# Attention pieces laid out afresh over the steps of a hand-ordered four-layer kernel

## The reference

```python
x = x + _L0(_gn(x))   # triplet attention: max and mean pools along three axes, 7x7 convolutions
                      # of them, sigmoid gates, the three gated branches weighted by a softmax
x = x + _L1(_gn(x))   # 3x3 convolution 256 -> 256, weights mixed from circulant projections
x = x + _L2(_gn(x))   # squeeze and excite: mean of a wavelet low band, two small matrices, sigmoid
x = x + _L3(_gn(x))   # shifted 8x8 window attention, 8 heads of 32, relative bias, mask
```

## Time and profile before

| | us |
|---|---|
| median of 3 runs | 3209.29 (3207.8 to 3211.7) |
| profiled execution | 3209.59 |
| its span | 3207.5 |
| PE, DVE, ACT, POOL busy | 2517.5, 2317.2, 1714.9, 1407.3 |
| mean granted clock of TensorE | 0.92 of full |

### The profile page before, as it was taken

How to read it: one execution, slowest core, us unless ns; L and a number is a source line. 1 busy time by engine, 2 the same in 40 slices (tenths; PEclk the granted TensorE clock), 3 DMA queues, 4 the chain that set the end, 5 groups by cost and what they waited for, 6 DMA issues and landing times. The chain is left out here.

```text
span 3207.5 us, 68136 instructions
## 1 busy us (share of the span) xinstructions
PE 2517.5 (78%) x27316; PEld 1422.3 (44%) x27316; DVE 2317.2 (72%) x4411; ACT 1714.9 (53%) x4448; POOL 1407.3 (44%) x1052
## 2 busy tenths in 40 slices
PE   0266769897888879798888979898788969798666
PEld 0232345444544446444544446444544445444343
DVE  4968676867778786878778786877678786776433
ACT  0221066545664476645764476635765376645765
POOL 4314552456335562456335562456435452454222
PEclk9977879998999989998999979998999989999899
DMA  5300310014000321014000321014010231011100
GB/s 149 104 2 14 108 58 28 21 60 145 28 28 27 118 68 41 21 60 145 28 28 27 103 83 41 21 60 145 22 34 27 73 113 41 21 47 54 41 28 34
DMA packets 91345, 184.50 MB, mean 58 GB/s; under 512 B 37510, under 2 KB 50454, under 8 KB 80406
## 3 DMA queue, kind: packets, MB, share of 16 engines
q1 hardware_dynamic: 88854, 177.78, 16.6%
q10 hardware_dynamic: 2176, 2.36, 0.3%
HBM read 107.23 MB, written 72.86 MB: 56 GB/s over the span
## 5 line engine op out<-in xcount | busy, mean ns | idle before, releaser
L1828 PE MATMUL F<-g_raw,cw_hi 128*128 128x512 f16 x2304 | 714.3, 393 | 62.0 <-DVE ytj L1361 25.5
L821 POOL TENSOR_TENSOR xs<-xs,rec 128x512 f32<-128x512 f32 x256 | 291.2, 1142 | 911.5 <-DVE rec L1615 910.8
L1081 ACT ACTIVATE xs<-xs,mx 128x64 f32<-128x64 f32 x2048 | 513.0, 336 | 166.4 <-DVE mx L1610 166.3
L1828 PE MATMUL F<-g_raw,cw_lo 128*128 128x512 f16 x1152 | 450.7, 391 | 0.0
L1828 PEld LDWEIGHTS F<-g_raw,cw_hi 128*128 128x128 f16 x2304 | 225.6, 100 | 342.9 <-issue 35.8
L1599 DVE TENSOR_TENSOR xs<-SP,bias 128x512 f32<-128x512 f32 (+2 forms) x384 | 182.1, 502 | 199.4 <-PE SP L1904 194.7
L1872 PE MATMUL QP<-tok_hi,qkv_hi 128*128 128x512 f16 x512 | 209.0, 408 | 98.2 <-DVE tok_lo L1584 44.9
L830 POOL TENSOR_TENSOR ot_lo<-ot,ot_hi 128x512 f16<-128x512 f32 x128 | 149.3, 1187 | 263.7 <-ACT ot_hi L1102 263.7
L1334 DVE SCALAR_TENSOR_TENSOR g_raw<-l0c,gn,g_raw 128x512 f16<-128x512 f32 x192 | 199.4, 1083 | 87.3 <-ACT g_raw L965 87.3
L965 ACT ACTIVATE g_raw<-l0c,gn 128x512 f16<-128x512 f32 x192 | 128.1, 716 | 232.2 <-DVE l0c L1327 83.3
L1614 DVE TENSOR_REDUCE sums<-xs 128x8 f32<-128x512 f32 x256 | 172.0, 672 | 89.6 <-ACT xs L1081 87.7
(11 more groups left out here) (268 smaller groups left out, 5798.2 us busy)
## 6 DMA issues: line engine op xcount, KB each, us to landing
X<-in_x SPq DMA_DIRECT2D x32, 1024.0 KB, 7.2
scratch_x<-X SPq DMA_DIRECT2D x32, 1024.0 KB, 8.4
xs<-scratch_x SPq DMA_DIRECT2D x56, 512.0 KB, 3.7
out_x<-xs SPq DMA_DIRECT2D x56, 512.0 KB, 2.7
...
```

The costliest lines, as they stand in the source:

```text
L821: G.tensor_tensor(keyed(sc[:, u % 4, :]), keyed(sc[:, u % 4, :]), rec[:, u % 4, :].unsqueeze(2).to_broadcast([P, 8, TOK]), ALU.mult).then_ ...
L1081: last = S.activation(keys, keys, ACT.Exp, bias=mx[:, u % 4, i:i + 1])
L1828: last = T.matmul(F[:, n % 2, :], wgt[:, ci, C3 * comp + dx, P * co:P * co + P], win[which], start=(ci == 0 and dx == 0 and j == 0), stop= ...
```

## The change

TURN, AHEAD and LAST_ROWS get new contents. Nothing else of the kernel is touched. Each letter stands as often per image in the new table as in the old, for each engine: PE Q64 S16 T32 W32; ACT Q48 K32 X32 T32 O8; DVE S32 T32 K16 A16; POOL N32 O8; SP L8 S8. Below is the diff cut to the entries of DVE and PE, the first of ACT, SP's, and AHEAD; POOL's entries, the rest of ACT's and LAST_ROWS are changed in the same way.

```diff
@@ -54,60 +54,60 @@
-    "SP": {"norm0a": "L", "band0": "S", "band3": "LS", "bandturn": "L", "hwmean1": "SL", "hwmean4": "S",
-        "gate6": "L", "lift3": "S", "conv6.0": "L", "conv7.0": "S", "conv12.1": "L", "conv16.0": "S",
-        "stats1": "L", "norm3c": "S"},
...
-    "ACT": {"norm0a": "Q", "norm0b": "XXKK", "norm0c": "XT", "reduce0": "TQQ", "reduce1": "TQT", "reduce2": "KQ",
...
-    "DVE": {"norm0a": "KK", "norm0b": "A", "norm0c": "TT", "reduce1": "T", "reduce3": "S", "reduce4": "TS",
-        "reduce5": "SKA", "reduce6": "AKTTS", "hwgate": "T", "hwrows": "SSSSKT", "band2": "TT", "band3": "KA",
-        "hwmean0": "A", "hwmean2": "T", "logits": "SSST", "mix": "AKT", "mixturn": "S", "gate0": "A",
-        "gate1": "K", "gate5": "T", "gate6": "T", "gate7": "SS", "gate10": "KA", "gate12": "KAT",
-        "gate13": "SSTT", "gate16": "T", "norm1c": "SS", "lift2": "ATS", "lift3": "A", "conv0.0": "KKT",
-        "conv2.0": "T", "conv2.1": "ST", "conv5.0": "S", "conv6.1": "ST", "conv9.1": "KA", "conv11.0": "T",
-        "conv12.0": "AK", "conv14.1": "S", "conv15.0": "S", "conv15.1": "TT", "conv18.0": "STS", "conv19.0": "K",
-        "conv20.0": "KA", "conv21.0": "STS", "conv21.1": "T", "conv22.1": "A", "squeeze": "T", "norm3a": "SS",
-        "norm3b": "STS", "coefs": "A"},
-    "PE": {"norm0b": "QT", "norm0c": "Q", "reduce0": "TW", "reduce1": "QTWQ", "reduce2": "TQW", "reduce3": "SWQ",
-        "reduce4": "Q", "reduce5": "TQS", "reduce6": "WQQ", "reduce7": "TQW", "hwgate": "TQ", "hwrows": "WQTS",
-        "band0": "QW", "band1": "SQ", "bandturn": "Q", "hwmean0": "T", "hwmean1": "QW", "hwmean2": "TQ",
-        "hwmean3": "Q", "hwmean4": "TWT", "hwmean5": "Q", "hwmean7": "QWSWQSQ", "mix": "QT", "mixturn": "Q",
-        "gate0": "WT", "gate3": "Q", "gate5": "Q", "gate6": "Q", "gate7": "TQ", "gate8": "SW", "gate9": "QTWW",
-        "gate10": "QQ", "gate12": "Q", "gate13": "S", "gate15": "Q", "gate17": "TWQTQWTQ", "norm1a": "TW",
-        "norm1b": "W", "lift2": "SQQ", "lift3": "QS", "conv0.1": "TQ", "conv1.0": "Q", "conv2.1": "QQW",
-        "conv3.1": "TTQ", "conv4.1": "W", "conv5.0": "SQWT", "conv5.1": "WQ", "conv8.1": "Q", "conv10.0": "T",
-        "conv10.1": "S", "conv11.1": "Q", "conv12.1": "TW", "conv13.1": "Q", "conv15.1": "WQ", "conv16.0": "Q",
-        "conv16.1": "Q", "conv17.0": "Q", "conv17.1": "ST", "conv18.0": "TW", "conv18.1": "W", "conv19.0": "Q",
-        "conv19.1": "Q", "conv21.0": "SQ", "conv22.1": "T", "conv23.1": "QQQTQ", "norm2b": "W", "stats0": "W",
-        "norm2c": "T", "squeeze": "S", "excite": "WT", "norm3a": "W", "stats2": "Q", "norm3c": "SQQ"},
+    "SP": {"reduce3": "LL", "reduce7": "S", "hwconv": "L", "band2": "S", "bandturn": "L", "mix": "S",
+        "gate7": "L", "gate14": "S", "conv0.1": "LS", "conv11.1": "L", "conv12.0": "S", "conv14.1": "L",
+        "conv17.0": "S", "norm3a": "S"},
...
+    "ACT": {"norm0b": "K", "norm0c": "TKKX", "reduce0": "Q", "reduce1": "QTQ", "reduce2": "TKQ", "reduce3": "X",
...
+    "DVE": {"norm0c": "AKKTA", "reduce1": "TT", "reduce3": "SS", "reduce4": "ST", "reduce5": "T",
+        "reduce6": "SAKKAT", "reduce7": "T", "band1": "SSTSS", "band2": "K", "bandcopy": "ATK", "bandturn": "A",
+        "hwmean1": "T", "hwmean5": "T", "hwmean7": "S", "logits": "ST", "mix": "S", "mixturn": "A",
+        "gate1": "KKA", "gate2": "T", "gate3": "S", "gate4": "T", "gate5": "T", "gate7": "SST", "gate10": "S",
+        "gate12": "AKKA", "gate14": "T", "gate17": "STT", "norm1b": "S", "lift1": "S", "conv0.0": "A",
+        "conv0.1": "T", "conv2.0": "KKAT", "conv2.1": "STS", "conv4.0": "T", "conv5.0": "S", "conv6.0": "TS",
+        "conv11.0": "A", "conv13.0": "KSTTK", "conv14.0": "S", "conv14.1": "A", "conv17.1": "TSS",
+        "conv19.0": "KT", "conv19.1": "A", "conv20.0": "KT", "conv21.0": "SST", "conv21.1": "T", "conv22.1": "A",
+        "excite": "SS", "norm3b": "TS", "norm3c": "S"},
+    "PE": {"norm0b": "QQ", "reduce0": "QT", "reduce1": "Q", "reduce2": "QWQT", "reduce3": "STQ",
+        "reduce4": "WSWW", "reduce5": "TQ", "reduce6": "QWTQ", "zpool": "QWTQ", "hwgate": "QT",
+        "hwrows": "QWWQSQ", "band1": "S", "band2": "Q", "bandturn": "QT", "hwmean1": "Q", "hwmean2": "T",
+        "hwmean3": "QW", "hwmean4": "Q", "hwmean5": "W", "hwmean6": "QT", "hwmean7": "STWQW", "logits": "SQ",
+        "mix": "T", "mixturn": "Q", "gate1": "Q", "gate3": "Q", "gate4": "QW", "gate5": "QT", "gate6": "Q",
+        "gate7": "TSW", "gate8": "TQWW", "gate10": "SQ", "gate12": "Q", "gate14": "QQ", "gate16": "TQQQTW",
+        "lift2": "STWTW", "lift3": "WQ", "conv0.0": "QQ", "conv1.0": "SQ", "conv2.1": "QQ", "conv3.0": "T",
+        "conv3.1": "TQ", "conv4.0": "Q", "conv4.1": "STWWQTW", "conv5.1": "W", "conv9.1": "S", "conv10.1": "Q",
+        "conv11.0": "Q", "conv11.1": "T", "conv12.1": "WQ", "conv15.1": "QT", "conv16.0": "TQ", "conv16.1": "Q",
+        "conv17.0": "QWWSTQ", "conv17.1": "W", "conv18.1": "Q", "conv19.1": "Q", "conv20.1": "S", "conv21.0": "T",
+        "conv21.1": "Q", "conv23.1": "QTQQ", "norm2a": "W", "norm2b": "Q", "norm2c": "WT", "excite": "SW",
+        "norm3a": "TQW", "coefs": "SQ", "stats3": "T"},
...
-AHEAD = {"SP": {}, "POOL": {"N": 3, "O": 1}, "ACT": {"X": 3, "T": 4, "Q": 1, "O": 1}, "DVE": {"T": 3, "A": 1}, "PE": {"Q": 1, "T": 4, "W": 4}}
+AHEAD = {"SP": {"L": 1}, "POOL": {"N": 3, "O": 1}, "ACT": {"X": 1, "T": 4, "O": 1}, "DVE": {"T": 3, "A": 2}, "PE": {"Q": 2, "T": 3, "W": 4}}
```

More of the change, by code:

```diff
@@ L56 @@
 TURN = {
[41 rows of a table removed]
[10 rows of a table added]
+        "hwrows": "TQQK", "band1": "K", "band2": "KXQ", "band3": "OKXX", "bandturn": "XTQ", "hwmean0": "QTQK",
[8 rows of a table added]
+        "coefs": "XOXQ"},
[21 rows of a table added]
 }
-AHEAD = {"SP": {}, "POOL": {"N": 3, "O": 1}, "ACT": {"X": 3, "T": 4, "Q": 1, "O": 1}, "DVE": {"T": 3, "A": 1}, "PE": {"Q": 1, "T": 4, "W": 4}}
+AHEAD = {"SP": {"L": 1}, "POOL": {"N": 3, "O": 1}, "ACT": {"X": 1, "T": 4, "O": 1}, "DVE": {"T": 3, "A": 2}, "PE": {"Q": 2, "T": 3, "W": 4}}
 LAST_ROWS = {
-    "SP": "LSLSLSLSLSLSLLSLSS",
-    "POOL": "NNNONNNNONNNNONNNNNONNNNONNNNONNNNNONNNONNNO",
-    "ACT": ("QXKKTQXTQXQTQKTQOQKKXKXTXTXQQTQKQTKOQQXKXKTXKTQQXQTKQTOQXQXKKXXQTQKTQQTXKTQXOKQTKQTKXQQKTQXXXTQO"
-           "KQKTXTXQKQTQQXTQKOKKQXKTXTXTQQKQQXTXQOKTQKTKXQXQTQKQXTXQOXKQQKTQXTQTQTOKK"),
-    "DVE": ("TAKKTTSKSASTTSKATTSSATKSSATKTTSSTASAKTSTKTSSTTSAKKASTSSTSTTKASAKTTSTSSKSKATATTSSSTTKSAKAKTSKTSTS"
-           "STTATAAA"),
-    "PE": ("TQTQQWWQTQTWWQSQQSTQWTQTQWQTWQWQSQSQQTQTQWQWTQWTWSQQQSQQTQQTWQWSTQWTSWQTQTQQQWQWTQSSQWTWQTQWQTQT"
-           "QWQQWSTQWQTSQQWTWQTQQQSQSTWWQTQTQQQWTWQQSWTQSWTQQTWTWTWQWQQ"),
+    "SP": "LLSLSLSLSLSLSLSSLLS",
+    "POOL": "NNNONNNNNONNNNONNNNNONNONNNNNONNNONNNNNNONNO",
+    "ACT": ("TKTXKKTQQTQQQOKQXKKKXTQXQXTTQTQXQOQXKKKTXQTQXQTKQKTQXQKXOKXTXQTKQTQQKXTXQTQOKKXXQTKQQKTQTOQXKQXK"
+           "TXKXTTQQQTKQXQOXTQKXKTXTQKKQQTQQOQXKXKXKQKTTQTKQXQXXTOTQXTQKQXQTKQTOQK"),
+    "DVE": ("TKTATAKSSTAKAKSTSTTSSTASTASKKTTSSSKTKASATTTSSTTSSAKKATTSSSSTKTAKTATSSTSSTATKKATSSSAKTAKTTSTSSTSS"
+           "TKTTKAAAA"),
+    "PE": ("TQWQTTQQWQWQWQSQSQQTQWQQTTWTWQWSQQSQQTWQTQTQWQTWWSQQSTQQWQTQTQQSWTWQWTQTSQQWQQWQTQTSWWQSQTQQWTQT"
+           "WTQQQWSWQSTQQTWQTQWQQWTQWSQSQQQQTQTTWQQSSWTWTWQTQWWTQWTQWQQ"),
 }
```

## The result

The changed kernel took 3102.31 us (3099.99 to 3106.91, 4 runs) beside 3208.55 for the kernel before on the same chip: ratio 0.9674, 95% interval 0.9653 to 0.9695.

The account below looks back on a forecast made before the run. The prediction took PE as bound from pool matmul to first gate and from conv6 on, DVE as leading in the reductions and conv0 to conv5; its terms summed to -3.4 us a round, times 7 = -24: 3186 us, range 3161 to 3224.

Parts of the forecast that it names:

- Pool matmul to first gate: From 2D-pool matmul to first gate: one more Q on PE +1.3, logits 4.3 us earlier; -3.0 us a round.
- Reductions: reduce0 to reduce7: DVE, which leads there, gets two T more at 0.8 us each; +1.6 us a round.
- Gates: gate0 to gate14: S earlier saves about 1.5 us, two more Q on PE cost 1.0; -0.5 us a round.
- norm1 to conv5: norm1, lift, conv0 to conv5: up to 4.5 us freed, one third kept as DVE gets pieces back; -1.5 a round.
- sign of being wrong: Wrong if the logits are not earlier, or if gates and conv0 to conv5 each take over 2 us more.
- conv6 to conv23: PE's pieces cost +1.3 net, conv12's 2.19 us wait for DVE goes; -0.9 us a round.
- norm2 to norm0: Chain from band load to x's last fetch stays, an A leaves the way of the coefficients; -0.3 us a round.
- New waits: Anywhere in a round: one wait of 1.21 us that the old trace cannot show; +1.2 us a round.
- Tail: After the last front: a chain through single buffers, so no change; 0, bounds -4 and +4 us.
- The rule on weight loads: By weight-load busy time PE has room from conv6 on, so added Qs cost nothing: -6.0 us a round, 3168 us.
- Rival A: Removed waits are all kept and no new one comes: -6.6 us a round, 3163 us; chance 0.15.
- B: What one stretch gains the next gives back, so no change: 3209.6 us; chance 0.13.

Follow-up runs that it names:

- part_pool: New order only from hwconv to mixturn, the old one elsewhere; ratio 0.9947 to the kernel before.
- move_logits: Old table, with PE's last three letters QSQ behind the last hwmean matmul moved behind the logits matmuls; 3210.67 us, ratio 1.0006.
- probe_holes: Old table plus two unused DVE reductions in each of reduce1 and reduce2, where DVE waited for PE, in seven rounds; ratio 1.0016.
- probe_full: Old table plus two unused DVE reductions in each of reduce4 and reduce6, where DVE had no wait, in seven rounds; ratio 1.0072.
- part_gate: New order only from gate0 to gate14, the old one elsewhere; ratio 0.9987 to the kernel before.
- move_gate_q: Old table, with PE's Qs behind gate3, gate5, gate6, gate7 moved to gate2, gate3, gate5, gate6, and S from gate8 to gate7; 3213.08 us, 1.0017.
- less_conv0: New order everywhere but from gate15 to conv5.1, where the old one stands; 3110.32 us, ratio 0.9698 to the kernel before.
- part_conv6: New order only from conv6.0 to coefs, the old one elsewhere; ratio 0.998 to the kernel before.
- part_tail: New order only in the tail, the old one in all rounds; ratio 0.9973 to the kernel before.
- fronts_only: New order in all rounds, the old one in the tail; ratio 0.975 to the kernel before.
- join_over_norm0: New order from conv6.0 over the coefficients to zpool of the next round, the old one elsewhere; 3156.22 us, ratio 0.984.
- join_to_gate: New order from norm0a to gate14, the old one in the rest of the round and the tail; 3168.03 us, ratio 0.9876.
- the third: New order from norm0a to conv5.1, the old one from conv6.0 to the coefficients and in the tail (join_to_conv5); 3172.23 us, ratio 0.9884.

## Why the prediction was wrong

The direction was right and the size was a quarter of what came. The waits that the forecast named did go; it left out others that were as long, and charged pieces for time that was free.

*Pool matmul to first gate, -3.0; found -5.4.* Mechanism right: the logits come 0.2 us behind the pooled means, 4.7 us sooner after the last hwmean matmul, and 4.2 of it last to the first gate, against 4.3 forecast; part_pool has them too. Wrong was the +1.3 for the Q in the band, which stayed at 31.5 and 31.3 us. Left out were two T fewer on PE behind hwmean0 to hwmean6: by my own price 1.0, and hwmean fell by 1.0, in part_pool as well. move_logits shows that bringing the logits forward is worth nothing by itself: the pieces must also leave the way to the first gate, where the new list has two Q fewer and one T more.

*Reductions, +1.6; found -3.6.* The step that failed most, with 5.2 of the 10.1 us a round: I charged two T their full length because DVE leads, and saw in the 8.7 us of idle time only room for them. I did not read from the trace what DVE waited for: 9.1 us for transposes that PE's own list held up. probe_holes shows that work put into these waits costs a quarter of its length, probe_full that it costs its length elsewhere; the new lists removed 6.1 of 7.5 us of such waits a round. That PE's list does it, and not the other engines' beside it, is read from the trace.

*Gates, -0.5; found -3.4.* Of the 2.67 us 2.3 went, where 1.5 were forecast. The 2.8 us that DVE waited for ACT's tokens went too, and the sum has no term for them. The two Q that I let cost 1.0 cost nothing: part_gate has 35.6 us with them. move_gate_q shows that the earlier S alone is not it.

*norm1 to conv5, -1.5; found +1.9.* The 4.5 us ahead of conv0 were nearly met (-3.1), the price was not: I kept a third of the 4.5 as net, and conv0 to conv5 got 5.0 longer, where over 2 us more there and at the gates was to be a sign of being wrong (the gates went the other way). I had counted DVE's and PE's pieces there and not ACT's. ACT's new list has more of them there (K3 X3 Q5 T4 for X2 T3 Q4), and DVE waits 5.3 us more for ACT's half. The sum lies within its bounds (-4.5 and +3), on the wrong side of zero. In the new order the stretch's list costs nothing all the same (less_conv0).

*conv6 to conv23, -0.9; found -1.1.* Right in the sum, by luck in part. conv12 waits 0.5 us instead of 2.19, but new waits of 0.7 and 0.2 stand before conv7 and conv8: conv6 to conv11 gained 0.4 where 2.2 were forecast. conv12 to conv17 take 38.2 us, +1.7 for 3.0 us of pieces (granted clock 1.00, 0.95 before), and conv18 to conv23 gained 2.4 where 1.7 were forecast.

*norm2 to norm0, -0.3; found -1.9.* Failed. I said that no attention piece stands in the chain from SP's band load to the last fetch; the S behind conv16.0 stands ahead of it, and I had looked only at the pieces that moved behind stats1. The trace shows the earlier fetch, in part_conv6 too. What it can be worth is small, 0.6 us of DVE's wait a round; 0.9 more is the A behind coefs, which also had no term. SP's move alone was not tried.

*New waits, +1.2.* The new list has such waits (1.26 and 6.2 us), but fewer in sum: PE idles 47.4 us a round (55.0), DVE 78.3 (87.4), ACT 139.1 (152.0), mean of images 3 to 7. Booking one on top, with no wait booked as removed in the reductions, was wrong.

*Tail, 0; found -8.3*, beyond the bound of -4. part_tail shows 4.9 of it with the old rounds, fronts_only 16.6 with the new ones. Which pieces do it is not shown.

*The rule on weight loads* (the Trainium skill, Perfetto Trace Analysis, Identifying the Most-Contended Engine). Weight-load busy time is 46.48 of 97.30 us from conv6 on, as before, and conv12 to conv17 did get 1.7 us longer with 3.0 us of pieces more, while the gates and the band took theirs for nothing. The trace bears the rule out in the latter two and not in the former. That section of the Trainium skill names the share of peak FLOPs beside weight-load time, which the forecast left out.

*Rival A* (all removed waits are kept, 3163 us) was the nearest and still 60 us off. *B*, that one stretch gains and the next gives back, is what happens to every part alone, and not to the whole. That is what the forecast lacked: I priced stretches by the pieces in them, with borders at which each had its old neighbours. join_over_norm0 (51 us where its parts give 11) and the whole (105, parts 28) show that gains add when their neighbours are new too, and join_to_gate (40, parts 25) leans that way; the third moved its border to a dearer place. Why the whole order needs each piece where it stands is not shown piece by piece.
